# New slot tables for the engines of a two-layer attention and expert kernel, and a second set for its last two batches

## The chip, the core and the metric

The kernel runs on one core of one Trainium2 chip. The core has five engines with an instruction queue each, worked off in order: TensorE (PE, its weight loads shown as PEld), VectorE (DVE), ScalarE (ACT), GpSimd (POOL) and SyncE (SP, which here only issues DMAs). They meet only in semaphores. The metric is the device time of one launch in microseconds; lower is better.

## The reference, cut to what matters

```python
x = x + L0_xattn(layernorm(x), ctx)   # softmax(theta ctx . phi x) . g x, layer norm over all, relu, out_w, + ctx
x = x + L0_ffn(layernorm(x))          # base_w x + 2 of 8 low-rank experts (lora), gates by softmax
x = x + L1_xattn(layernorm(x), ctx)   # 8 heads of 32 rows: softmax(q k) v, keys and values from ctx
x = x + L1_moe(layernorm(x))          # router 512x64, 8 of 64 experts a row, silu(gate)*up, down, scatter-add
```

There are 16 batches of 256 rows by 512 columns, all float32.

## The kernel before, in words

**Two stages.** The first stage runs the first three layers and the routing, batch by batch, and writes each normed row with its 64 weights into the slots of its 8 experts in HBM (`slot_rows`). The second stage (from about 1222 us) runs over the 64 experts: it loads an expert's 256 slots and weights, multiplies them, and adds the results into `out_rows` in HBM.

**The order of the first stage.** It is written out in tables, one per engine. A table gives each event a position in slots. A batch has 32 slots: in slot n, TensorE does ("key", n), the product whose exponent ScalarE takes (`key_chunk`, profile line L665), and ("score", n+20), the product whose row maximum VectorE takes ahead of time (`score_chunk`, L656; maximum L1190). `schedule` turns tables into one list per engine, sorted by position; events of one position keep an order of kind and batch. Only the order counts: an engine does its list in order and waits at an event until its semaphores allow it.

- Preparation of batch b (tables `TENSOR`, `SCALAR`, `VECTOR`, `GPSIMD`, `SYNC`): an event stands at 32b - 64 + its number. `ctx` and `x` load the batch (L413, L404). `theta`, `phi`, `g`, `s0`-`s3` (L577), `t0`-`t3`, `lat`, `mean`, `o0`, `o1` are the first layer; `x0`, `x1`, `lora`, `b00`-`b13`, `gated`, `f0`, `f1` the second. `xn40`, `xn41`, `q_hi`, `q_lo`, `k_hi`, `k_lo` make the operands of the third. `k0`-`k3` and `q0`-`q3` on SP are three DMAs each that stack them for heads 0/4, 1/5, 2/6, 3/7 (L419); the first score of a head waits for its stacks.
- Two quads of 16 slots make a batch. When a quad's 16 scores are reduced, the maxima are turned (`max`, L689), split by ScalarE and VectorE, and SP copies them (`max_rows`, L429, 8 KB each) as two more rows of the stack. The quad's first key waits for both (`max_in`). `sums`, `turn`, `inv`, `add` finish a quad and add it to the batch's rows.
- Dispatch of batch b (tables `_OUT`, at 32(b+1) + number): `stats0`, `stats1`, `rstd`, `rows0`, `rows1` norm the finished rows (L1231), `x0`, `x1` (L720), `route` (L729), `exp`, `top0`-`top2`, `place`, `place0`-`place2` route them and give the slots (`slot_i`, L1290); 16 `send` events on POOL write the rows (indirect DMAs, L1431); `out` on SP writes the residual stream.
- Fills: slots of HBM that no row reaches must hold zeros. SP writes 577 KB for each of the 64 experts (`fill`, L463), at -18, -16.56, -15.13 ... with 1.44 slots between them, the last at 72.6.

**PSUM banks.** Banks 0 to 4 belong to keys, scores and weighted sums. All other events share banks 5 to 7; a planner in `build` walks TensorE's list and gives each stage the bank whose last reader stands earliest. A stage waits until that reader is done.

Of the kernel before, what the change touches and what calls it, by code (L numbers as in the profile page):

```python
# [31 lines left out]
class Count:  # L32
# [5 lines left out]
    def up(self, by=1):  # L38
# [5 lines left out]


PREPARE = 64
TENSOR = {"theta": 10.5, "phi": 10.5, "g": 12, "s0": 11, "t0": 18, "lat0": 20, "s1": 11, "t1": 19, "lat1": 23.25,
# [3 lines left out]
SCALAR = {"xn0": 8, "xn1": 9.25, "xn20": 34.75, "xn21": 34.75, "xn40": 42.5, "xn41": 42.5, "theta": 10.75,  # L51
# [4 lines left out]
VECTOR = {"stats0": 4.75, "stats1": 6, "s0": 11.25, "r0": 12.25, "s1": 11.25, "r1": 12.5, "s2": 11.5, "r2": 14,  # L56
# [27 lines left out]

def schedule(dims, prepare, tail, maxima, dispatch, core):

    B, HALF, NHEAD, C = dims["B"], dims["HALF"], dims["NHEAD"], dims["T"] // P
    H4 = NHEAD // HALF  # L90
    QUAD, SLOTS = C * H4, NHEAD * C
    AHEAD = LEAD * H4
    out = []
    if "fill" in core:
        out += [(FILL_FROM + n * FILL_SLOTS / dims["NEXP"] - PREPARE, 0, ("fill", n)) for n in range(dims["NEXP"])]
    for n in range(B * SLOTS):
        if "key" in core:
            out.append((n, 0, ("key", n)))
        if "score" in core:
            out.append((n - AHEAD, 1, ("score", n)))  # L100
        if "add" in core and n // H4 % C == 1:
            out.append((n + 1, 2, ("add", n)))
# [33 lines left out]
def build(nc, a, out, slots_dram, dims):  # L136
    B, HALF, T, L, NHEAD, DQ, NE, NEXP, CAP, TOPK, NRANK = (
        dims[k] for k in ("B", "HALF", "T", "L", "NHEAD", "DQ", "NE", "NEXP", "CAP", "TOPK", "NRANK"))
# [21 lines left out]
    tensor_order = schedule(dims, TENSOR, TENSOR_TAIL, TENSOR_MAX, TENSOR_OUT, ("key", "score", "weighted"))  # L160
    scalar_order = schedule(dims, SCALAR, SCALAR_TAIL, SCALAR_MAX, SCALAR_OUT, ("key",))
    vector_order = schedule(dims, VECTOR, VECTOR_TAIL, VECTOR_MAX, VECTOR_OUT, ("score",))
    gpsimd_order = schedule(dims, GPSIMD, {}, {}, GPSIMD_OUT, ("add",))
    sync_order = schedule(dims, SYNC, {}, SYNC_MAX, SYNC_OUT, ("fill",))

# [16 lines left out]
    with stack:  # L182
        def sem(name):
            return stack.enter_context(nc.semaphore(name))
# [51 lines left out]
        lat_rstd = sem("lat_rstd")  # L236
# [3 lines left out]
        gate_exp = sem("gate_exp")  # L240
# [33 lines left out]
        def A(name, shape, dt=F32):  # L274
            return sb(name, shape, dt, small)
# [31 lines left out]
        theta = A("theta", [P, T])  # L307
        phi = A("phi", [P, T])
# [3 lines left out]
        lat = theta  # L312
# [22 lines left out]
        top2 = A("top2", [P, HALF, 8])  # L335
# [5 lines left out]
        gated = A("gated", [P, HALF, NF])  # L341
# [1190 lines left out]
```

## Time and profile before

| | us |
|---|---|
| median of 3 runs | 1825.39 (1823.33 to 1825.6) |
| the profiled execution's own time | 1832.02 |
| its span | 1830.3 |
| TensorE busy | 1651.0 (90%) |
| VectorE, ScalarE, GpSimd busy | 1198.1, 1003.3, 964.8 |

The span runs from the first instruction of the program to its last. In the profile's forty slices TensorE is at 5 to 8 tenths in the first four (to 183 us), at 9 from there to 1098 us, at 6, 2 and 9 tenths in the three slices from 1144 us, and at 9 to the end.

### The profile page before, as it was taken

The numbers are of one execution on the slowest core, as the hardware profiler recorded it, in microseconds if no ns is written. First come the engines' busy times: TensorE is split into PE (matmuls) and PEld (weight loads), VectorE is DVE, ScalarE is ACT, GpSimd is POOL, SyncE is SP. The second block draws the span as 40 slices with busy tenths as digits, with TensorE's granted clock in tenths as the row PEclk, the third lists the DMA queues.
The fourth block names the chain that finished last, engine by engine and source line by source line (L and its number), as shares of the span: only waits on it lengthen the run. The fifth ranks groups of instructions, "written<-read, shape, count | busy, mean of one in ns | idle before, by whom it ended". The sixth has DMA issues, their size and how long they took to land. (4 is left out here: it accounts for less than half of the span.)

```text
span 1830.3 us, 26026 instructions
## 1 busy us (share of the span) xinstructions
PE 1651.0 (90%) x8576; PEld 1075.1 (59%) x8576; DVE 1198.1 (65%) x2706; ACT 1003.3 (55%) x1970; POOL 964.8 (53%) x882
## 2 busy tenths in 40 slices
PE   5878899999999999999999989629999999999994
PEld 2434454554554554554555544329888888888884
DVE  2555577777787777787787776317766666657662
ACT  3435556666656666656656644315555555555552
POOL 3121232563563563563564555756666666666665
PEclk8979999999999999999999999759999999999997
DMA  3679663533533533523431330159999999999985
GB/s 101 187 235 315 195 226 90 184 110 124 184 116 114 169 100 109 155 84 93 129 91 59 98 84 18 33 167 242 243 256 245 253 255 246 252 248 255 259 226 79
DMA packets 139732, 303.32 MB, mean 166 GB/s; under 512 B 27385, under 2 KB 29305, under 8 KB 139598
## 3 DMA queue, kind: packets, MB, share of 16 engines
q1 hardware_dynamic: 100686, 230.23, 40.4%
q0 software_dynamic: 38912, 71.43, 17.9%
q8 instruction: 69, 1.13, 0.3%
q14 instruction: 65, 0.53, 0.1%
HBM read 132.60 MB, written 155.91 MB: 158 GB/s over the span
## 5 line engine op out<-in xcount | busy, mean ns | idle before, releaser
L1190 DVE TENSOR_REDUCE max_col<-bank 128x1 f32<-128x512 f32 x512 | 345.0, 685 | 159.5 <-PE bank L656 157.0
L946 ACT ACTIVATE p_t<-bank 128x512 f32<-128x512 f32 x512 | 299.0, 596 | 198.0 <-PE bank L665 194.7
L1478 POOL DMA_INDIRECT out_rows<-y_slots,row_ids x128 | 228.7, 1787 | 203.9 <-DMA out_rows<-y_slots,row_ids 158.7
L1419 POOL TENSOR_TENSOR p_sum<-p_t 128x512 f32<-128x512 f32 x128 | 167.3, 1318 | 307.7 <-ACT p_t L946 306.6
L1431 POOL DMA_INDIRECT slot_rows<-row,slot_i x256 | 265.8, 1038 | 72.0 <-issue 71.9
L665 PE MATMUL bank<-q_stack,k_stack 98*128 98x512 f32 x512 | 274.3, 536 | 16.3 <-DMA q_stack<-max_lo 15.3
L656 PE MATMUL bank<-k_stack,q_stack 96*128 96x512 f32 x512 | 213.4, 418 | 22.9 <-issue 13.9
L665 PEld LDWEIGHTS bank<-q_stack,k_stack 98*128 98x128 f32 x512 | 98.4, 193 | 174.5 <-issue 152.1
L1468 POOL TENSOR_TENSOR down_lo<-down,down_hi 96x1024 fp32r<-96x1024 f32 x64 | 188.4, 2944 | 16.0 <-DVE down_hi L1350 16.0
L1319 DVE TENSOR_TENSOR x_slots_t_lo<-bank,x_slots_t_hi 128x512 fp32r<-128x512 f32 x128 | 88.3, 690 | 156.2 <-ACT x_slots_t_hi L1003 156.1
L785 PE MATMUL bank<-gate_up_hi,x_slots_t_hi 128*128 128x384 f32 x512 | 186.9, 365 | 0.7 <-DVE x_slots_t_lo L1319 0.5
L787 PE MATMUL bank<-gate_up_hi,x_slots_t_lo 128*128 128x384 f32 x512 | 175.8, 343 | 0.0
L786 PE MATMUL bank<-gate_up_lo,x_slots_t_hi 128*128 128x384 f32 x512 | 175.7, 343 | 0.0
L1023 ACT ACTIVATE y_slots<-bank,x_slots 128x512 f32<-128x512 f32 x128 | 88.1, 688 | 132.1 <-PE bank L809 132.1
L774 PE MATMUL bank<-ident,x_slots 128*128 128x128 f32 x512 | 80.7, 281 | 64.1 <-DMA x_slots<-slot_rows 64.1
L678 PE MATMUL bank<-p_t,v_t 128*32 128x512 f32 x1024 | 137.7, 610 | 0.0
L1340 DVE TENSOR_TENSOR gate_up_lo<-gate_up,gate_up_hi 128x768 fp32r<-128x768 f32 x128 | 132.2, 1034 | 7.0 <-ACT gate_up_hi L1033 7.0
L656 PEld LDWEIGHTS bank<-k_stack,q_stack 96*128 96x128 f32 x512 | 99.5, 194 | 62.8 <-issue 40.2
L637 PE MATMUL bank<-base_w,x_t 128*128 128x512 f32 x256 | 123.0, 603 | 0.0
L774 PEld LDWEIGHTS bank<-ident,x_slots 128*128 128x128 f32 x512 | 62.6, 143 | 89.7 <-DMA x_slots<-slot_rows 43.2
L1033 ACT CAST gate_up_hi<-gate_up 128x768 fp32r<-128x768 f32 x128 | 105.3, 824 | 15.1 <-DMA down<-in_down 15.1
L807 PE MATMUL bank<-down_hi,hidden_t_hi 96*128 96x512 f32 x256 | 112.0, 437 | 1.8 <-POOL down_lo L1468 1.8
(175 smaller groups left out, 3304.2 us busy)
## 6 DMA issues: line engine op xcount, KB each, us to landing
gate_up<-in_gate_up SPq DMA_DIRECT2D x64, 768.0 KB, 6.5
slot_rows<-row SPq DMA_DIRECT2D x64, 577.0 KB, 7.3
x_slots<-slot_rows SPq DMA_DIRECT2D x64, 577.0 KB, 4.5
k_stack<-prob SPq DMA_DIRECT2D x192, 128.0 KB, 2.4
down<-in_down SPq DMA_DIRECT2D x64, 384.0 KB, 7.4
q_stack<-x_t SPq DMA_DIRECT2D x128, 128.0 KB, 3.3
x<-in_x SPq DMA_DIRECT2D x16, 512.0 KB, 3.7
ctx<-in_ctx SPq DMA_DIRECT2D x16, 512.0 KB, 3.9
```

Of the source, the lines that this page charges most:

```text
L656: e.matmul(psum[2 + n % 2][:, :], q_st[b % 2][0:SK, head, c * P:(c + 1) * P], k_st[b % 2][0:SK, head, :], start=True, stop=True).then_inc( ...
L665: e.matmul(psum[n % 2][:, :], k_st[b % 2][0:SKM, head, j * P:(j + 1) * P], q_st[b % 2][0:SKM, head, :], start=True, stop=True).then_inc(fu ...
L774: m = e.transpose(psum[u % 2][:, c * P:(c + 1) * P], xe[i][:, s, c * P:(c + 1) * P], ident[:, :])
L785: e.matmul(bk[:, 0:2 * INNER], xt_hi[u % 3][:, c, :], gu_hi[nw][:, c, :], start=c == 0, stop=False)
L786: e.matmul(bk[:, 0:2 * INNER], xt_hi[u % 3][:, c, :], gu_lo[nw][:, c, :], start=False, stop=False)
L787: m = e.matmul(bk[:, 0:2 * INNER], xt_lo[u % 3][:, c, :], gu_hi[nw][:, c, :], start=False, stop=c == C - 1)
L946: e.activation(p_t[step % 2][:, h, :], psum[n % 2][:, :], ACT.Exp, scale=SCALE).then_inc(free[n % 2], 1)
L1190: e.tensor_reduce(max_col[quad % 2][:, h, c:c + 1], psum[2 + n % 2][:, :], X, ALU.max, negate=True).then_inc(free[2 + n % 2], 1)
L1419: e.tensor_tensor(p_sum[:, h, :], p_t[(step - 1) % 2][:, h, :], p_t[step % 2][:, h, :], ALU.add).then_inc(p_sum_ok, 1)
L1431: e.indirect_dma_start(out=slots_dram, in_=rows[b % 2][:, k, :], in_offset=None, out_offset=bass.IndirectOffsetOnAxis(ap=slot_i[b % 2][:, ...
L1468: e.tensor_tensor(dn_lo[nw][:, :, :], dn[i][:, :, :], dn_hi[nw][:, :, :].bitcast(F32), ALU.subtract).then_inc(dn_lo_ok, 1)
L1478: e.indirect_dma_start(out=out, out_offset=bass.IndirectOffsetOnAxis(ap=row_ids[e_ % NI][:, q, :].bitcast(U32), axis=0), in_=ye[e_ % NY][: ...
```

## The change

Every table gets new numbers. `SYNC` moves `x`, `ctx`, `q3`, `max` and `out` by 6.5 to 9 slots to the back, `k` and `q0`-`q2` hardly at all. A second set of dispatch tables (`_LATE`) holds for batches 14 and 15: their `x0` on TensorE stands at 74.5 instead of 41. `schedule` takes it as one more argument. No instruction is added or removed; `FILL_FROM` and the fills' positions stay. `GPSIMD_LATE` has rstd 42.25 and send 78.25.

```diff
-TENSOR = {... "s0": 11, "t0": 18, ... "s1": 11, "s2": 11.25, "s3": 13, ... "b02": 40.25, "gated": 40.5, "v0": 41.5, "v1": 42.75,
-          "theta": 10.5, "phi": 10.5, "g": 12 ...}
+TENSOR = {... "s0": 11.25, "t0": 14.75, ... "s1": 11.25, "s2": 11.25, "s3": 11.25, ... "b02": 41, "gated": 41, "v0": 41.75, "v1": 42.5,
+          "theta": 10, "phi": 10.5, "g": 12 ...}
-SCALAR = {... "xn40": 42.5, "xn41": 42.5, "theta": 10.75, "phi": 10.75, "n0": 12.75, "n3": 16.25, "k_hi0": 25.25, "k_hi1": 28, "q_hi0": 42.5 ...}
+SCALAR = {... "xn40": 42.5, "xn41": 42.5, "theta": 10.25, "phi": 11, "n0": 12.25, "n3": 13.25, "k_hi0": 38.5, "k_hi1": 38.75, "q_hi0": 42.5 ...}
-GPSIMD = {"rstd": 7.25, "res0": 9.5, "res1": 10.75, "lat_rstd": 28, "rstd2": 34.5, "rstd4": 42.25}
-SYNC = {"ctx": -11.75, "x": -5.5, "k0": 41.5, "k1": 42.5, "k2": 42.75, "k3": 42.75, "q0": 43, "q1": 43, "q2": 45.5,
-        "q3": 45.75}
+GPSIMD = {"rstd": 7.75, "res0": 10, "res1": 10, "lat_rstd": 28, "rstd2": 32, "rstd4": 42.25}
+SYNC = {"ctx": -5, "x": 2, "k0": 41, "k1": 41.25, "k2": 41.75, "k3": 42.5, "q0": 43, "q1": 43, "q2": 43, "q3": 52.25}
 
-TENSOR_OUT = {"x0": 41, "x1": 41, "route": 42, "place": 44}
-SCALAR_OUT = {"x0": 41.25, "x1": 41.75, "exp": 42.5}
-GPSIMD_OUT = {"rstd": 25, "send": 65}
-SYNC_OUT = {"out": 22}
+TENSOR_OUT = {"x0": 42.25, "x1": 42.5, "route": 43, "place": 46.25}
+SCALAR_OUT = {"x0": 42.5, "x1": 42.75, "exp": 43.5}
+GPSIMD_OUT = {"rstd": 22.25, "send": 67.5}
+SYNC_OUT = {"out": 31}
+
+LATE = 2
+TENSOR_LATE = {"x0": 74.5, "x1": 76, "route": 76.5, "place": 77.75}
+SCALAR_LATE = {"x0": 75, "x1": 76.25, "exp": 77}
+VECTOR_LATE = {"stats0": 34.25, "stats1": 36.5, "rows0": 46, "rows1": 48.5, "peak": 76.75, ... "place2": 78}
 ...
-SYNC_MAX = {"max": 5.75}
+SYNC_MAX = {"max": 13}
 ...
-        for what, o in dispatch.items():
+        for what, o in (dispatch if b < B - LATE else late).items():
```

## Rows read from the trace of the kernel before

**Rows 1.** Windows: us, busy us of PE, PEld, DVE, ACT, POOL, clock, DMA share, GB/s

```profile
76.00:106.00 30.00, 16.01 (x51) 8.07 (x50) 18.80 (x37) 7.86 (x15) 2.10 (x6) 0.77 1.03 360
300.00:1100.00 800.00, 780.17 (x4046) 413.86 (x4042) 605.67 (x1527) 493.66 (x968) 428.81 (x497) 0.99 0.39 116
1161.00:1222.00 61.00, 17.11 (x97) 13.92 (x95) 17.37 (x68) 8.23 (x19) 45.43 (x49) 0.58 0.25 72
1222.00:1831.00 609.00, 550.08 (x3072) 495.23 (x3072) 374.40 (x637) 319.25 (x638) 383.86 (x192) 0.95 0.91 236
```

**Rows 2.** Waits of PE, 40 to 300 us: total us, times, longest

```profile
PE bank L665 <- DMA q_stack<-max_lo: 15.3, 4, 8.2
```

**Rows 3.** Timeline of PE: start, us; idle before and releaser in brackets

```profile
105.76 0.77 PE L665 MATMUL bank<-q_stack,k_stack 98*128 98x512 f32 x1 [8.20 <-DMA q_stack<-max_lo]
...
150.60 0.76 PE L665 MATMUL bank<-q_stack,k_stack 98*128 98x512 f32 x1 [3.59 <-DMA q_stack<-max_lo]
...
222.49 0.77 PE L665 MATMUL bank<-q_stack,k_stack 98*128 98x512 f32 x1 [2.83 <-DMA q_stack<-max_lo]
```

**Rows 4.** Timeline of SP's DMA issues

```profile
76.09 5.47 SPq L463 DMA_DIRECT2D slot_rows<-row  x5
...
95.55 1.04 SPq L429 DMA_DIRECT2D q_stack<-max_hi  x1
...
133.51 0.59 SPq L419 DMA_DIRECT2D q_stack<-x_t  x1
...
145.22 1.14 SPq L429 DMA_DIRECT2D q_stack<-max_hi  x1
...
217.07 1.46 SPq L429 DMA_DIRECT2D q_stack<-max_hi  x1
```

**Rows 5.** Line L463 from 75 to 105 us: issues, and time from issue to landing

```profile
L463 SPq DMA_DIRECT2D slot_rows<-row x20: 507/1145/1843, 76.1 to 103.9; - x20
...
DMA to landing us min/median/max: 4.2/8.9/10.8
```

**Rows 6.** Line L429, the same, at 90 to 100 us

```profile
DMA to landing us min/median/max: 9.0/9.3/9.6
```

**Rows 7.** Line L429, the same, at 170 to 174 us

```profile
DMA to landing us min/median/max: 1.8/1.8/1.8
```

**Rows 8.** Timeline around the first score of a batch

```profile
416.76 0.79 PE L665 MATMUL bank<-q_stack,k_stack 98*128 98x512 f32 x1
...
418.67 0.47 PE L656 MATMUL bank<-k_stack,q_stack 96*128 96x512 f32 x1 [1.11 <-issue]
...
422.40 1.02 PE L577 MATMUL bank<-phi,theta 128*128 128x512 f32 x2
```

**Rows 9.** Timeline before it, of another batch

```profile
814.23 1.08 ACT L976 COPY x_t<-bank 128x512 f32<-128x512 f32 x2 [1.96 <-PE bank L720]
...
819.44 1.12 ACT L932 CAST x_t<-xn 128x512 fp32r<-128x512 f32 x2
...
820.46 1.88 PE L562 MATMUL bank<-xn,phi_w 128*128 128x512 f32 x4
```

**Rows 10.** Group of keys, 300 to 1100 us: busy us, mean ns, idle before

```profile
L665 PE MATMUL bank<-q_stack,k_stack 98*128 98x512 f32 x376 | 201.5, 536 | 0.0
```

**Rows 11.** Line L665 from 60 to 260 us: ns shortest, median, longest

```profile
L665 PE MATMUL bank<-q_stack,k_stack x72: 392/500/803, 105.8 to 258.3; 98*128 98x512 f32 x72
```

**Rows 12.** Timeline of the end of the first stage

```profile
1163.68 1.09 PE L720 MATMUL bank<-ident,row 128*128 128x128 f32 x8
...
1165.95 1.97 PE L729 MATMUL bank<-route_w,x_t 128*128 128x64 f32 x16 [1.19 <-ACT x_t L976]
...
1175.52 0.17 DVE L1290 TENSOR_SCALAR slot_i<-slot 128x16 int32<-128x16 f32 x1
...
1179.27 1.07 POOL L1431 DMA_INDIRECT slot_rows<-row,slot_i  x1 [0.19 <-issue]
...
1183.61 3.64 PE L729 MATMUL bank<-route_w,x_t 128*128 128x64 f32 x16 [0.72 <-issue]
```

More of the change, by code:

```diff
@@ L46 @@
 PREPARE = 64
-TENSOR = {"theta": 10.5, "phi": 10.5, "g": 12, "s0": 11, "t0": 18, "lat0": 20, "s1": 11, "t1": 19, "lat1": 23.25,
[3 rows of a table removed]
-SCALAR = {"xn0": 8, "xn1": 9.25, "xn20": 34.75, "xn21": 34.75, "xn40": 42.5, "xn41": 42.5, "theta": 10.75,
[4 rows of a table removed]
-VECTOR = {"stats0": 4.75, "stats1": 6, "s0": 11.25, "r0": 12.25, "s1": 11.25, "r1": 12.5, "s2": 11.5, "r2": 14,
[3 rows of a table removed]
-GPSIMD = {"rstd": 7.25, "res0": 9.5, "res1": 10.75, "lat_rstd": 28, "rstd2": 34.5, "rstd4": 42.25}
-SYNC = {"ctx": -11.75, "x": -5.5, "k0": 41.5, "k1": 42.5, "k2": 42.75, "k3": 42.75, "q0": 43, "q1": 43, "q2": 45.5,
-        "q3": 45.75}
@@ L64 @@
-TENSOR_OUT = {"x0": 41, "x1": 41, "route": 42, "place": 44}
-SCALAR_OUT = {"x0": 41.25, "x1": 41.75, "exp": 42.5}
-VECTOR_OUT = {"stats0": 4.75, "stats1": 22.75, "rows0": 25.75, "rows1": 25.75, "peak": 42.25, "top0": 42.75,
-              "top1": 42.75, "top2": 42.75, "place0": 45.75, "place1": 46, "place2": 46}
-GPSIMD_OUT = {"rstd": 25, "send": 65}
-SYNC_OUT = {"out": 22}
-TENSOR_TAIL = {"sums0": -2.5, "sums2": -1.75, "sums1": 1, "turn": 11, "inv": 15.75}
-SCALAR_TAIL = {"heads": 4.5, "sums": 6.5, "expand": 12.75}
@@ L73 @@
-VECTOR_TAIL = {"turn": 11.25, "inv": 16, "add": 17.5}
+TENSOR = {"theta": 10, "phi": 10.5, "g": 12, "s0": 11.25, "t0": 14.75, "lat0": 20, "s1": 11.25, "t1": 16.75,
[3 rows of a table added]
+          "lora": 39.5, "gated": 41}
+SCALAR = {"xn0": 8.5, "xn1": 9.75, "xn20": 34, "xn21": 34.75, "xn40": 42.5, "xn41": 42.5, "theta": 10.25, "phi": 11,
[4 rows of a table added]
+VECTOR = {"stats0": 4.75, "stats1": 5.5, "s0": 11.5, "r0": 12, "s1": 11.5, "r1": 12, "s2": 11.5, "r2": 12, "s3": 11.5,
[3 rows of a table added]
+GPSIMD = {"rstd": 7.75, "res0": 10, "res1": 10, "lat_rstd": 28, "rstd2": 32, "rstd4": 42.25}
@@ new lines @@
+SYNC = {"ctx": -5, "x": 2, "k0": 41, "k1": 41.25, "k2": 41.75, "k3": 42.5, "q0": 43, "q1": 43, "q2": 43, "q3": 52.25}
+TENSOR_OUT = {"x0": 42.25, "x1": 42.5, "route": 43, "place": 46.25}
+SCALAR_OUT = {"x0": 42.5, "x1": 42.75, "exp": 43.5}
+VECTOR_OUT = {"stats0": 20.25, "stats1": 20.5, "rows0": 25.5, "rows1": 25.5, "peak": 43.25, "top0": 43.75, "top1": 44,
+              "top2": 44, "place0": 46.5, "place1": 46.5, "place2": 46.5}
+GPSIMD_OUT = {"rstd": 22.25, "send": 67.5}
+SYNC_OUT = {"out": 31}
@@ new lines @@
+LATE = 2
+TENSOR_LATE = {"x0": 74.5, "x1": 76, "route": 76.5, "place": 77.75}
+SCALAR_LATE = {"x0": 75, "x1": 76.25, "exp": 77}
+VECTOR_LATE = {"stats0": 34.25, "stats1": 36.5, "rows0": 46, "rows1": 48.5, "peak": 76.75, "top0": 77.25, "top1": 77.5,
+               "top2": 77.5, "place0": 78, "place1": 78, "place2": 78}
+GPSIMD_LATE = {"rstd": 42.25, "send": 78.25}
+SYNC_LATE = {"out": 37.5}
+TENSOR_TAIL = {"sums0": -2.25, "sums2": -2.25, "sums1": 0.25, "turn": 11, "inv": 15.5}
+SCALAR_TAIL = {"heads": 4.75, "sums": 7, "expand": 14.75}
@@ L75 @@
+VECTOR_TAIL = {"turn": 11.5, "inv": 18, "add": 18.5}
 TENSOR_MAX = {"max": 1.25}
@@ L77, with schedule @@
 VECTOR_MAX = {"max_lo": 1.75}
-SYNC_MAX = {"max": 5.75}
-WEIGHTED = 6.25
+SYNC_MAX = {"max": 13}
+WEIGHTED = 6.5
 LEAD = 5
 FILL_FROM, FILL_SLOTS = 46, 92
-def schedule(dims, prepare, tail, maxima, dispatch, core):
+def schedule(dims, prepare, tail, maxima, dispatch, late, core):
     B, HALF, NHEAD, C = dims["B"], dims["HALF"], dims["NHEAD"], dims["T"] // P
@@ L158, in build @@
     BC = NHEAD * C
[L160 to L164, printed above, removed]
+    tensor_order = schedule(dims, TENSOR, TENSOR_TAIL, TENSOR_MAX, TENSOR_OUT, TENSOR_LATE, ("key", "score", "weighted"))
+    scalar_order = schedule(dims, SCALAR, SCALAR_TAIL, SCALAR_MAX, SCALAR_OUT, SCALAR_LATE, ("key",))
+    vector_order = schedule(dims, VECTOR, VECTOR_TAIL, VECTOR_MAX, VECTOR_OUT, VECTOR_LATE, ("score",))
+    gpsimd_order = schedule(dims, GPSIMD, {}, {}, GPSIMD_OUT, GPSIMD_LATE, ("add",))
+    sync_order = schedule(dims, SYNC, {}, SYNC_MAX, SYNC_OUT, SYNC_LATE, ("fill",))
     read_at = {}
```

20 rows, old and new, of tables (SCALAR, TENSOR, VECTOR) are left out of this document.

## The prediction, made before the result was known

> **What bounds the kernel now.** I first cut the span into windows [rows 1]. From 300 to 1100 us TensorE is busy 780 of 800 us at a granted clock of 0.99: it bounds the steady part, and 19.8 us of idle time in some 12 batches, 1.65 us a batch, are what a better order could take from it outright. Waits inside a matmul's modelled length are not in that: keys last 536 ns in the mean [rows 10], and with nothing to hold them about 400 (the shortest 392 [rows 11]). The second stage is at 0.91 of the DMA engines from 1222 us on; nothing of it is touched. Two stretches are bounded by something else. From 76 to 106 us TensorE is busy 16 of 30 us while the DMA engines show 1.03 and 360 GB/s: the fills saturate them. From 1161 to 1222 us POOL is busy 45 of 61 us with 49 instructions, the sends, and TensorE 17.
>
> Then I read what TensorE waits for at the start. Its longest kind of wait there, 15.3 us in four times, is for the small DMAs of the quad's maxima [rows 2], and it stands before the first key of quads 0, 1 and 3 (8.20, 3.59, 2.83 us) [rows 3].
>
> **Step 1, the start: SP's order against the fills.** I merged both sets of positions. In the steady part SP's order stays what it is: max, k, q, max, ctx, out, x. Only against the fills, which keep their positions, do the moved events change place. `max` of quad 0 goes from 0.75 to 8 and so behind five more fills (n = 14 to 18); of quad 1 from 16.75 to 24, five more (25 to 29); of quad 3 from 48.75 to 56, five more. `q3` goes from just behind `q2` to behind five fills for batch 0 and six for batches 1 and 2.
>
> What five fills cost: a fill is 577 KB, at 360 GB/s [rows 1] 1.64 us, so five are 8.2 us. That such a backlog stands before a later DMA is in the trace: 20 fills, issued from 76.1 to 103.9 us, took 4.2 us from issue to landing at first and up to 10.8 [rows 5], and the 8 KB of quad 0's maxima issued in their midst took 9.0 to 9.6 us [rows 6], where the same DMAs took 1.8 us with nothing ahead [rows 7].
>
> - Quad 0: SP came to `max` at 95.55 us [rows 4], its key started at 105.76 [rows 3]. Behind five more fills it lands 8.2 us later. The fills begin earlier by `q3`'s three DMAs, 1.9 us of issue, but these then stand behind five fills and add 1.1 us of transfer: 8.2 + 1.1 - 1.9 = 7.4 us. `q3` itself lands at about 87 us instead of 77, which holds score 3 and all behind it for some 9 us, but the maxima are then ready at about 100 us, before SP gets to them at about 102: it costs nothing on top.
> - Quad 1: `q0` is issued at 133.5 us [rows 4]; `q0` to `q2` take nine issues, 5.8 us; then six fills (9.8 us) and `q3` (1.1), three fills (4.9): with the 3.5 us to the first landing the maxima land at about 158.6 - 1 = 157.6 us on the old time base, where the key started at 150.6 [rows 3]: 7.0 us.
> - Quad 2: `max` was issued into an empty queue [rows 7], and its key came some 10 us later; five more fills are gone by then. Nothing.
> - Quad 3: as quad 1, nine fills and `q3` behind `q2`: 8.1 us behind the old 222.49 us [rows 3].
> - Quad 4: SP stands at `x` of batch 4 for rows of batch 0 before it, in both orders, with four fills behind; nothing.
>
> Sum 22.5 us. TensorE takes its list in order, so each pause shifts all behind it. Some of it comes back, since ScalarE, VectorE and POOL catch up in a pause and later small waits for them shrink; the quads' other waits are 0.7 to 2 us each. I take 3.5 us back: +19. Bounds: 0, if DMAs of 8 KB get past the backlog, and +26, if nothing comes back and the lower clock after each pause (0.77 in 76 to 106 us [rows 1]) lasts longer.
>
> The Trainium skill bears on this in DMA: Bandwidth & Descriptors, section Queues, rings and completion order: each DMA engine consumes descriptors in ring order, but completion is not first in, first out per issuing engine, since a later DMA on few engines need not wait for an earlier one's other engines. The 9.0 to 9.6 us [rows 6] speak for the queue and against overtaking. By overtaking the sum would be 1828, by the queue 1846.
>
> **Step 2, the steady batches.** The first score of a batch waits for `q0`, 1.11 us at 418.67 us [rows 8], and `s3`, two matmuls with 0.86 us from start to start, stood behind it; now it stands ahead and fills the wait. `v0` no longer stands behind `x0` and `x1` of the dispatch, which saves 0.4 us. So -1.3 us a batch at best. Against it: the planner now gives `x0` and `x1` of the dispatch the same bank, where they had two. ScalarE reads `x0` only behind `xn40`, `xn41`, `q_hi0` and `q_hi1`, which end at 819.44 + 1.12 = 820.56 us [rows 9]; with a copy of 0.6 us the bank is free at 821.2, and TensorE, with the phi group (1.88 us at 820.46 [rows 9]) now drawn forward, would be there at 819.9: +1.3. `route`, the `turn` that VectorE reads only behind `peak`, and `s1` and `s2`, whose banks hang on these reads, come 0.7 us late: +2.0 at worst. `rstd4` on POOL has five operations of about 1.3 us between it and the last add as before (two sends and two residual adds and a norm, for three sends, one add and a norm), so `q0` comes no sooner. The moved `t0` to `t3`, `n0` to `n3` and `k_hi` lie where neither view shows TensorE waiting: zero, hidden by keys and scores; without that cover a 0.7 us operation each. Over 13 batches the ends are -17 and +26 us. I take 0, since the two wait places are of one size.
>
> **Step 3, the end.** POOL sends 48 times (batches 13, 14 and 15) from 1157 us on, 1.28 us each, with only one gap: 1.75 us behind the send at 1179.27 [rows 12]. So nothing that makes slots sooner counts; what makes them late does. Before, the dispatch of batch 14 stood ahead of quad 31's `turn`: transposes at 1163.68 us, slots at 1175.7, and POOL came to batch 14's sends at 1179.27 [rows 12]. Now `turn`, `inv` and the tail's copies come first, so the transposes start at about 1168.3: slots at 1175.7 + 4.6 - 0.6 (the `turn` that stood in between) = 1179.7. The route took 1.97 us at 1165.95 and 3.64 at 1183.61 with the clock at its lower level [rows 12], and it would now run at 1170 or later: 1181.4. POOL waits 0.4 to 2.1 us. Batch 15's rows come before its sends are due. `rstd` of batch 14 is now amid the sends, which moves it and adds none. I take +1.5; the ends are -1.5 (the gap of 1.75 us goes) and +3.5.
>
> **The sum.** 19 + 0 + 1.5 = +20.5 us: the profiled execution's span of 1830.3 would be 1850.8 and its own time of 1832.0 1852.5. It stood 6.6 us above the median of the runs; on the median's base, 1825.4 + 20.5 = 1846 us.
>
> **Rivals.**
> - The steady part packs better: the pauses' cost of step 1 stays, but the new order takes the 1.65 us of idle time a batch [rows 1] and a third of the stretch in the keys (376 times 136 ns, 51 us [rows 10]): over 13.5 batches 22 + 19 = 41 us. It would be 1846 - 41 + bank waits of some 15 = 1820, faster. For it: `s3` in the wait of `q0`. Against it: the bank chain. It decides from 1.6 us a batch.
> - The backlog doesn't count for 8 KB: with 1.8 us to landing [rows 7] and SP at `max` at 102.5 us quad 0's key would start at about 105, as before; the start costs at most 2 us, the whole 1828, which is no change. The page named in step 1 allows this much, since completion needn't follow the order of issue.
> - The bank chain has no cover: step 2 at +1.5 us a batch, +20, so 1866.
> - The end gets shorter, since batch 15's rows no longer stand behind batch 14's routing in quad 31's tail: POOL is the bound, so at most the 1.75 us. This changes no sign.
>
> **How the numbers follow.** A change of 0.2%, 3.7 us, is about what can be told here. Forecast (1834 to 1858) 0.55; packs better 0.17; no backlog 0.08; bank chain 0.15; else, slower by other waits, 0.05. So faster 0.17, same 0.08, slower 0.75. The range takes the forecast's own, half of the faster case and most of the bank chain: 1822 to 1865.
>
> **What would show it.** Waits for q_stack<-max_lo before 300 us of 35 us and more instead of 15.3; first keys at about 113, 165 and 245 us; L429 issued at 102 us; a first batch of sends of batch 14 with POOL idle for slot_i before it; batches 5 to 15 within 1 us of 66 to 68 us each. Wrong it is if the first key starts before 108 us, or if a steady batch changes by over 1.5 us.

## The result and the profile after

| | us | ratio to the kernel before |
|---|---|---|
| before, median of 4 runs | 1824.9 (1823.3 to 1825.6) | |
| after, median of 4 runs | 1847.1 (1841.7 to 1855.8) | 1.0127 (0.95 interval 1.0085 to 1.017) |
| after, profiled execution | 1841.7, span 1840.0 | |

The change made the kernel 22 us slower; 1846 was predicted. The two profiled executions lie only 9.7 us apart in their spans, since that of before stood above its median and that of after below. So each trace is cut at the last send of the first stage: it starts at 1220.9 us before and at 1241.4 after, 20.5 us later. What is left behind it is 609.3 us before and 598.5 after; no instruction of the second stage differs, and the last section shows that this part scatters.

Windows of the changed kernel, columns as in [rows 1]:

```profile
76.00:106.00 30.00, 18.36 (x44) 9.77 (x44) 17.20 (x32) 3.33 (x6) 0.88 (x3) 0.66 1.03 353
300.00:1100.00 800.00, 784.78 (x4067) 412.36 (x4066) 602.36 (x1531) 492.15 (x978) 408.58 (x485) 1.00 0.38 114
```

The DMA engines are as full at the start as they were (1.03 in both), and in the steady part TensorE is busy 785 of 800 us instead of 780. What TensorE waits for between 40 and 300 us has changed; of [rows 2] the one line is now two:

```profile
PE bank L664 <- issue: 22.3, 3, 8.3
PE bank L673 <- DMA q_stack<-max_lo: 13.7, 4, 4.4
```

L664 is the score, L673 the key. Where these waits stand, in the timeline of TensorE (before in [rows 3]):

```profile
81.54 1.19 PE L664 MATMUL bank<-k_stack,q_stack 96*128 96x512 f32 x2 [7.16 <-issue]
...
108.18 0.76 PE L673 MATMUL bank<-q_stack,k_stack 98*128 98x512 f32 x1 [4.28 <-DMA q_stack<-max_lo]
...
156.46 0.77 PE L664 MATMUL bank<-k_stack,q_stack 96*128 96x512 f32 x1 [6.87 <-issue]
...
161.65 0.76 PE L673 MATMUL bank<-q_stack,k_stack 98*128 98x512 f32 x1 [4.42 <-DMA q_stack<-max_lo]
...
235.70 0.77 PE L664 MATMUL bank<-k_stack,q_stack 96*128 96x512 f32 x1 [8.28 <-issue]
...
241.45 0.76 PE L673 MATMUL bank<-q_stack,k_stack 98*128 98x512 f32 x1 [4.12 <-DMA q_stack<-max_lo]
```

The three pauses ahead of a score are those of the first score that needs `q3`, in batches 0, 1 and 2: 22.3 us where the kernel before has 2.6. The profile names no releaser for them ("issue"); that they are waits for `q3` is shown by a_q3_back below, where they fall to 1.9 us. And SP's issues (before in [rows 4]):

```profile
62.45 0.59 SPq L427 DMA_DIRECT2D q_stack<-x_t  x1
...
74.38 1.28 SPq L427 DMA_DIRECT2D q_stack<-x_t  x1
...
77.13 1.40 SPq L427 DMA_DIRECT2D q_stack<-x_t  x1
...
98.06 1.08 SPq L437 DMA_DIRECT2D q_stack<-max_hi  x1
```

The first of these lines is the first copy of `q0` of batch 0. No fill stands ahead of it in either kernel, so the change of SP's order does not reach it. In the kernel before it stands at

```profile
67.78 0.58 SPq L419 DMA_DIRECT2D q_stack<-x_t  x1
```

So this execution was 5.3 us ahead before the first fill was issued. That is scatter: after_again, a_no_late and a_no_late_again are the same program up to there, and have this copy at 65.3, 62.7 and 66.4 us. Where the start is measured below, it is therefore counted from this copy too.

For the rest one table does, read from the traces of all kernels: where the turned maxima (`max` on TensorE) of four quads and the last send start, in us. Quad 4 is the end of the start, quads 5 to 30 are the steady part, and the last column but one is the end of the stage, from quad 30's maxima to the last send.

| kernel | quad 0 | quad 4 | quad 5 | quad 30 | last send | steady | end |
|---|---|---|---|---|---|---|---|
| before | 89.9 | 242.1 | 285.7 | 1115.2 | 1220.9 | 829.5 | 105.7 |
| after | 96.5 | 260.3 | 304.1 | 1137.3 | 1241.4 | 833.2 | 104.1 |
| a_sp_before | 90.3 | 240.2 | 284.5 | 1118.9 | 1222.6 | 834.4 | 103.7 |
| b_sp_after | 98.1 | 263.6 | 309.6 | 1136.5 | 1242.5 | 826.9 | 106.0 |
| a_q3_back | 91.6 | 269.0 | 315.6 | 1147.6 | 1251.7 | 832.0 | 104.1 |
| a_max_back | 100.5 | 251.5 | 294.6 | 1140.3 | 1246.7 | 845.7 | 106.4 |
| a_fills_grouped | 90.5 | 220.3 | 268.0 | 1173.2 | 1291.2 | 905.2 | 118.0 |
| a_fills_again | 91.2 | 220.5 | 268.1 | 1174.2 | 1292.4 | 906.1 | 118.2 |
| b_fills_grouped | 87.9 | 218.1 | 263.1 | 1090.0 | 1205.9 | 826.9 | 115.9 |
| b_fills_again | 87.8 | 218.1 | 263.1 | 1089.2 | 1206.8 | 826.1 | 117.6 |
| after_again | 99.1 | 259.5 | 303.8 | 1205.9 | 1324.2 | 902.1 | 118.3 |
| a_sp_gated | 91.1 | 241.1 | 286.3 | 1190.7 | 1309.1 | 904.4 | 118.4 |
| a_no_late, a_no_late_again | 96.8, 99.5 | 260.1, 262.7 | 304.1, 306.8 | 1199.3, 1212.2 | 1319.5, 1332.2 | 895.2, 905.4 | 120.2, 120.0 |

After against before: +18.4 us up to quad 5, +3.7 from there to quad 30, and -1.6 to the last send. Their sum is the 20.5. The 18.4 hold 23.7 us of delay behind the first copy of `q0` and the 5.3 us that this execution was ahead at it. The kernel before has one trace only, from the first group of runs; all kernels are compared with that one.

### The profile page after: what moved, and what is told of

It is laid out like the page before. It is cut to its first block, busy times and chain, and to the rows that moved or that the text cites. A ratio compares the mean times of both kernels' runs of the same rounds, so it can differ in the third digit from the quotient of the medians.

```text
span 1840.0 us, 26037 instructions
## 1 busy us (share of the span) xinstructions
PE 1647.4 (90%) x8576; PEld 1067.8 (58%) x8576; DVE 1191.8 (65%) x2706; ACT 994.2 (54%) x1970; POOL 947.6 (52%) x882
## 4 chain that ended last, share of the span: by engine, by line
PE 44%; DMA 20%; issue 12%; POOL 10%; SPq 6%; DVE 6%; ACT 3%; POOLq 0%; ACTq 0%; DVEq 0%
DMA out_rows<-y_slots,row_ids 16%; PE bank L673 5%; PE bank L686 5%; PE bank L664 5%; POOL slot_rows L1439 4%; PE bank L606 3%; SPq L427 3%; SPq L471 2%; PE bank L708 2%; PE bank L645 2%; POOL p_sum L1427 2%; PE bank L585 2%; PE bank L650 2%; PE bank L599 2%; PE bank L701 2%
## 5 line engine op out<-in xcount | busy, mean ns | idle before, releaser
L1198 DVE TENSOR_REDUCE max_col<-bank 128x1 f32<-128x512 f32 x512 | 340.9, 683 | 160.9 <-PE bank L664 159.0
L1486 POOL DMA_INDIRECT out_rows<-y_slots,row_ids x128 | 221.9, 1733 | 200.5 <-DMA out_rows<-y_slots,row_ids 157.6
L1427 POOL TENSOR_TENSOR p_sum<-p_t 128x512 f32<-128x512 f32 x128 | 162.9, 1280 | 294.4 <-ACT p_t L954 292.9
L1439 POOL DMA_INDIRECT slot_rows<-row,slot_i x256 | 260.2, 1016 | 79.1 <-issue 78.1
L673 PE MATMUL bank<-q_stack,k_stack 98*128 98x512 f32 x512 | 268.2, 525 | 16.0 <-DMA q_stack<-max_lo 13.7
L664 PE MATMUL bank<-k_stack,q_stack 96*128 96x512 f32 x512 | 216.4, 425 | 33.3 <-issue 25.8
L1476 POOL TENSOR_TENSOR down_lo<-down,down_hi 96x1024 fp32r<-96x1024 f32 x64 | 188.6, 2948 | 15.3 <-DVE down_hi L1358 15.3
L673 PEld LDWEIGHTS bank<-q_stack,k_stack 98*128 98x128 f32 x512 | 98.6, 193 | 157.0 <-issue 131.9
L664 PEld LDWEIGHTS bank<-k_stack,q_stack 96*128 96x128 f32 x512 | 101.1, 198 | 72.5 <-issue 47.6
L1348 DVE TENSOR_TENSOR gate_up_lo<-gate_up,gate_up_hi 128x768 fp32r<-128x768 f32 x128 | 136.0, 1063 | 7.0 <-ACT gate_up_hi L1041 7.0
```

The source lines that it names most:

```text
L664: e.matmul(psum[2 + n % 2][:, :], q_st[b % 2][0:SK, head, c * P:(c + 1) * P], k_st[b % 2][0:SK, head, :], start=True, stop=True).then_inc( ...
L673: e.matmul(psum[n % 2][:, :], k_st[b % 2][0:SKM, head, j * P:(j + 1) * P], q_st[b % 2][0:SKM, head, :], start=True, stop=True).then_inc(fu ...
L1198: e.tensor_reduce(max_col[quad % 2][:, h, c:c + 1], psum[2 + n % 2][:, :], X, ALU.max, negate=True).then_inc(free[2 + n % 2], 1)
L1427: e.tensor_tensor(p_sum[:, h, :], p_t[(step - 1) % 2][:, h, :], p_t[step % 2][:, h, :], ALU.add).then_inc(p_sum_ok, 1)
L1439: e.indirect_dma_start(out=slots_dram, in_=rows[b % 2][:, k, :], in_offset=None, out_offset=bass.IndirectOffsetOnAxis(ap=slot_i[b % 2][:, ...
L1476: e.tensor_tensor(dn_lo[nw][:, :, :], dn[i][:, :, :], dn_hi[nw][:, :, :].bitcast(F32), ALU.subtract).then_inc(dn_lo_ok, 1)
```

## The experiments

Names with a_ start from the changed kernel, with b_ from the kernel before. a_sp_before, b_sp_after, a_q3_back and a_max_back shared a chip (before: median 1829.8). The two fills_grouped, a_no_late and a_sp_gated ran on another (before: 1845.0), the four named again on a third (before: 1831.6). The kernel before scatters by 11 to 22 us within each of these groups, so the traces decide more than the times.

**a_sp_before.**

```diff
-SYNC = {"ctx": -5, "x": 2, "k0": 41, ... "q2": 43, "q3": 52.25}
+SYNC = {"ctx": -11.75, "x": -5.5, "k0": 41.5, ... "q2": 45.5, "q3": 45.75}
-SYNC_OUT = {"out": 31}   -SYNC_MAX = {"max": 13}
+SYNC_OUT = {"out": 22}   +SYNC_MAX = {"max": 5.75}
```

> The changed kernel with SP's three tables (SYNC, SYNC_MAX, SYNC_OUT) as before; the other engines keep the new ones, and batches 14 and 15 their second set. Theory: the place of q3 and of the maxima's copies among the fills is the whole cost, some 18 us by the shift of quad 4 between the two traces (242.1 to 260.3 us at its turned maxima). Then the time is 1847 - 18 = 1829 (1825 to 1833), and no score waits over 2 us before 260 us. Rival, the other engines' tables cost as well: it stays above 1836. Rival, they gain and SP's order hid it (the waits ahead of scores fell from 15.8 to 7.2 us between 300 and 1100 us): below 1822.

Measured: 1832.1, ratio 1.0014 (0.9991 to 1.0037). Waits of TensorE, 40 to 300 us:

```profile
PE bank L674 <- DMA q_stack<-max_lo: 14.1, 4, 6.3
PE bank L665 <- issue: 1.9, 2, 1.7
```

The start is that of the kernel before (quad 4 at 240.2 against 242.1; counted from the first copy of `q0`, 174.6 against 174.3), and with it the 20 us are gone. The other tables leave +4.9 us in the steady part and -2.0 in the end.

**b_sp_after.** The reverse: these three tables of the changed kernel in the kernel before.

> The kernel before with SP's three tables from the changed one, nothing else. Theory: 1825 + 18 = 1843 (1839 to 1848), with waits of about 7, 7 and 8 us ahead of the score that needs q3 in batches 0, 1 and 2 and the turned maxima of quad 4 at about 260 us instead of 242. Rival, other tables cost too: below 1836. That SP's order costs only together with the new order of the other engines would show as no change, 1825.

Measured: 1852.1, ratio 1.0114 (1.0066 to 1.0161), 22 us above the kernel before.

```profile
PE bank L655 <- issue: 24.7, 3, 10.4
PE bank L664 <- DMA q_stack<-max_lo: 15.7, 4, 5.6
```

SP's order alone makes the loss of the start, with either order of the other engines. Quad 4 is 21.5 us late here and 18.2 in the changed kernel; counted from the first copy of `q0` it is 24.2 and 23.5, so the other tables make no difference that can be told.

**a_q3_back.** Only `"q3": 52.25` to `45.75` in the changed kernel.

> The changed kernel with q3 at 45.75 as before, so ahead of the fills; the maxima stay behind five more fills. The working of the prediction says that the maxima alone set the first key: it then starts at about 112 us, the waits for the maxima rise from 13.7 to some 35 us, those of scores for q3 go, and the time stays at 1847 (1842 to 1852). Rival, the 22 us of waits for q3 are the cost and the maxima's place costs nothing: 1847 - 18 = 1829.

Measured: 1862.5, ratio 1.0162 (1.0107 to 1.0217). Moving `q3` forward brought no gain. The last send starts 10.3 us later than in the changed kernel's trace, but 6.1 of these stand already at the first copy of `q0` (68.5 instead of 62.4 us), which the edit doesn't reach; and the ratio's interval overlaps that of the changed kernel. The waits ahead of the scores are gone (1.9 us instead of 22.3). The pauses ahead of the keys:

```profile
PE bank L673 <- DMA q_stack<-max_lo: 44.2, 4, 16.0
```

```profile
115.22 0.77 PE L673 MATMUL bank<-q_stack,k_stack 98*128 98x512 f32 x1 [16.00 <-DMA q_stack<-max_lo]
...
170.76 0.77 PE L673 MATMUL bank<-q_stack,k_stack 98*128 98x512 f32 x1 [13.29 <-DMA q_stack<-max_lo]
...
249.67 0.76 PE L673 MATMUL bank<-q_stack,k_stack 98*128 98x512 f32 x1 [12.85 <-DMA q_stack<-max_lo]
```

These three keys are 7.8, 9.7 and 10.0 us longer on hold than in [rows 3]. That is the prediction's own mechanism, bare, and about as large as its 8.2 us for five fills. Most of it is that SP comes to the copies later, since each fill's issue takes some 1.2 us of SP's own time here:

```profile
76.79 12.15 SPq L471 DMA_DIRECT2D slot_rows<-row  x10
```

SP issued `max_lo` 7.7 us later than before at quad 0 (104.37 instead of 96.64 us, of which 0.7 stand already at `q0`), and 7.4 and 6.6 us later at quads 1 and 3, counted from the batch's own `q0`. The rest is the way from the issue to the key: 10.9 us instead of 9.1 at quad 0, 7.0 and 7.3 instead of 4.2 and 3.9 at the others.

**a_max_back.** Only `"max": 13` to `5.75` in the changed kernel.

> The changed kernel with the maxima's copies at 5.75 as before, so ahead of five fills; q3 stays behind five or six. If the maxima's place alone costs, 1829. If q3's place alone costs, 1847, with 22 us of waits ahead of scores. If each delays by its own, the waits for q3 stay at 22 us and those for the maxima fall from 13.7 to about 5, since the backlog drains while TensorE stands at q3: 1847 - 9 = 1838 (1834 to 1842).

Measured: 1850.2, ratio 1.0121 (1.0065 to 1.0177).

```profile
PE bank L664 <- issue: 21.9, 3, 8.5
```

The maxima are no longer among TensorE's waits there, and the 22 us for `q3` stand. At quad 4 the shift is 9.4 us (11.4 counted from the first copy of `q0`): each place delays by its own, as the third of the written expectations had it. The time missed that expectation because of the steady part, where this kernel loses 16 us against before: with `max` at 5.75 and `q3` at 52.25, SP reaches `q3` of the next batch only behind the maxima of the quad before it, at 641.46 us behind 640.22 in this timeline, and scores then wait in nearly every batch, 10.1 us in 12 times between 330 and 1110 us, against 3.5 in 4 for the changed kernel:

```profile
640.22 0.56 SPq L437 DMA_DIRECT2D q_stack<-max_hi  x1
...
641.46 0.65 SPq L427 DMA_DIRECT2D q_stack<-x_t  x1
```

```profile
PE bank L664 <- issue: 10.1, 12, 1.7
```

Between quads 5 and 30 TensorE is idle for 28.7 us here and 19.0 in the changed kernel. So this edit changed two things, and only its first 250 us are a clean test.

**b_fills_grouped and b_fills_again** (the same kernel, in the second and the third group).

```diff
-        out += [(FILL_FROM + n * FILL_SLOTS / dims["NEXP"] - PREPARE, 0, ("fill", n)) for n in range(dims["NEXP"])]
+        at = [p for p, n in FILL_AT for _ in range(n)]
+        out += [(at[n], 0, ("fill", n)) for n in range(dims["NEXP"])]
+FILL_AT = [(-18, 8), (0.8, 14), (16.8, 12), (32.8, 12), (48.8, 12), (64.8, 6)]
```

> The kernel before with its 64 fills grouped in the same way: 8 behind q3 of batch 0, then 14, 12, 12, 12, 6 right behind the maxima of quads 0 to 4. By the theory of the backlog the 15.3 us of waits for the maxima fall to about 5, the first key starts at about 99 us instead of 105.8: 1825 - 10 = 1815 (1810 to 1820), and within 6 us of the changed kernel with grouped fills. Rival: a group of 12 to 14 holds SP for some 15 us, so that x and ctx come late and give the gain back: 1825.

> The kernel before with grouped fills, once more, beside the others. On its first runs it was 25 us below the kernel before, of which its stage one accounts for 15 in the profile (last send at 1205.9 instead of 1220.9 us). If the 15 are the fills' and the rest scatter, it is 10 to 20 us below the kernel before here: 1805 to 1815 where that is at 1825. If it was the chip alone, no difference.

Measured: 1819.6 against 1845.0, ratio 0.986 (0.9812 to 0.9909), and 1809.3 against 1831.6, ratio 0.9883 (0.9821 to 0.9945). This version beats the kernel before in both groups, by 1.2 to 1.4%. The waits for the maxima, 15.3 us in [rows 2], are

```profile
PE bank L666 <- DMA q_stack<-max_lo: 2.1, 1, 2.1
```

and quad 4 comes 24.0 us sooner (22.0 counted from the first copy of `q0`), which is more than the 13 us of waits. One quad shows why. First the kernel before from quad 1's maxima to quad 2's, then the grouped one:

```profile
139.90:170.30 30.40, 25.80 (x124) 12.27 (x123) 12.40 (x26) 16.60 (x32) 5.03 (x4) 0.89 0.99 337
```

```profile
130.40:153.10 22.70, 22.70 (x125) 11.00 (x122) 12.23 (x26) 16.50 (x32) 5.04 (x4) 1.00 0.93 315
```

With the same matmuls, TensorE is idle for 4.6 us less and its busy time is 3.1 us shorter, at a granted clock of 1.00 instead of 0.89 (means of the stretch, of the two levels 1.2 and 2.4 GHz); 25.80 times 0.89 is 23.0, so the clock accounts for the difference in busy time. The clock is at its lower level in one piece of this stretch, 150.1 to 156.9 us, and that piece begins as the 3.6 us pause ahead of the key at 150.60 [rows 3] ends. So this pause is paid twice, as idle time and in the clock. Of the 24 us, 15.0 (14.1 in the repeat) arrive at the last send: the end takes 116 to 118 us instead of 105.7. POOL, which the prediction found busy with sends almost without a gap from 1157 us on, now stands for want of the last batches' rows:

```profile
1162.86 0.22 POOL L1372 TENSOR_SCALAR row_rstd<-row_mv 128x2 f32<-128x2 f32 x1 [6.82 <-DVE row_mv L1074]
```

**a_fills_grouped and a_fills_again.** The same grouping in the changed kernel, FILL_AT at -11.7, 8.05, 24.05, 40.05, 56.05, 72.05.

> The changed kernel with the same 64 fills in another place: 8 behind q3 of batch 0, and 14, 12, 12, 12, 6 right behind the maxima's copies of quads 0 to 4, so that in batches 1 to 3 no fill stands between a batch's q0 and its maxima. If the backlog of fills is what delays q3 and the maxima, the 36 us of waits for both fall to under 10 and turned maxima of quad 4 come before 240 us instead of 260: 1847 - 18 - 8 = 1821 (1815 to 1828). If SP's places of q3 and maxima cost in themselves, by other rows of SP, it stays at 1847.

> The changed kernel with grouped fills, the same as before. Stalls a matter of the chip: on one without them the time is that of the first forecast for it, 1821 (1815 to 1828), which is some 25 below the changed kernel of the same runs. Stalls made by the grouping: it is slow again, 1900, with the changed kernel at 1847.

Measured: 1903.5, ratio 1.0315 (1.0283 to 1.0348), and 1889.9, ratio 1.0329 (1.0257 to 1.0401). The times miss what was expected by some 80 and 70 us, but at quad 4 (220.3, 220.5 us) the kernel is where it was expected, 40 us ahead of the changed one and 2 from the kernel before with the same grouping. SP's places of `q3` and the maxima cost next to nothing in the start once no backlog of fills stands ahead. What was lost came behind quad 5.

**after_again.** The changed kernel itself, unchanged, in the third group.

> The changed kernel itself once more. In three runs of kernels with the new tables of the other engines TensorE stood still 5 to 10 us at the routing's 16 products of a batch (there VectorE and ScalarE waited 120.5 us in 20 times for the row maximum of the routing between 300 and 1150 us, against 32.5 us in 18 for the changed kernel's own profile), and each time took 60 to 90 us more. If that hangs on the chip that runs it, and on the new order of TensorE, the changed kernel does the same where those do, and is at 1847 or 20 above the kernel before of the same runs where they don't. If it hangs on the edits of those three (fills grouped, second set off, the gates' places), the changed kernel is 20 above the kernel before whatever they do.

Measured: 1934.6, ratio 1.0576 (1.0506 to 1.0646), so 103 us above the kernel before, where the first runs had 22. It is the same program with the same start (quad 5 at 303.8 against 304.1 us), and its steady part is 69 us longer. The first time it leaves the other trace (POOL, VectorE and TensorE):

```profile
361.73 1.09 POOL L1439 DMA_INDIRECT slot_rows<-row,slot_i  x1 [0.30 <-issue]
...
363.17 1.93 PE L737 MATMUL bank<-route_w,x_t 128*128 128x64 f32 x16
...
364.93 1.08 PE L585 MATMUL bank<-phi,theta 128*128 128x512 f32 x2
365.68 0.97 POOL L1439 DMA_INDIRECT slot_rows<-row,slot_i  x1 [0.30 <-issue]
...
369.51 0.97 POOL L1439 DMA_INDIRECT slot_rows<-row,slot_i  x1 [0.30 <-issue]
...
371.34 0.29 DVE L1246 TENSOR_REDUCE r_max<-bank 128x2 f32<-128x128 f32 x1 [7.72 <-remote]
```

The router's 16 products end at 365.1 us by the trace's model, and VectorE, which waits for them alone, starts at 371.34: TensorE's signal came 6.2 us late. TensorE then stands itself, 6.05 us here, since its next product needs a bank that VectorE reads only behind `r_max`. What VectorE and ScalarE waited for ahead of `r_max` and its reader, 300 to 1150 us, first here, then in the first profile of the same kernel:

```profile
  remote: 135.9, 20
```

```profile
  PE bank L737: 32.5, 18
```

It hangs on the new order of the engines together with the chip or the hour: a_fills_grouped, a_no_late and a_sp_gated have it, and the repeats; the changed kernel's first profile and the four kernels of the first group have it nowhere, VectorE starting 0.04 us behind the products each time; and b_fills_grouped and b_fills_again, run beside them, have it in none of the steady batches. POOL differs at that place. In the new order a row of eight sends stands back to back around the router's products. In the old one, as here in b_fills_again, single sends stand between adds:

```profile
381.49 1.30 POOL L1389 TENSOR_TENSOR x<-x,ctx 128x512 f32<-128x512 f32 x1
382.95 1.00 POOL L1432 DMA_INDIRECT slot_rows<-row,slot_i  x1 [0.17 <-issue]
...
383.45 1.90 PE L730 MATMUL bank<-route_w,x_t 128*128 128x64 f32 x16
384.02 0.22 POOL L1372 TENSOR_SCALAR row_rstd<-row_mv 128x2 f32<-128x2 f32 x1
...
385.38 0.29 DVE L1239 TENSOR_REDUCE r_max<-bank 128x2 f32<-128x128 f32 x1 [1.04 <-PE bank L730]
```

In after_again the batch before the first sends (router done at 297.9 us) is undisturbed. The 11 that follow, to 1109 us, are late by 1.5 to 7.4 us, 54.2 us together, of the 69 that its steady part is longer. SP's copies of `q` stand beside the router in the new order too, which would be a rival. But the one late signal of b_fills_again, 2.25 us at 1149.9 us (2.09 in b_fills_grouped), falls in the end of the stage, where POOL has sends in a row and SP issues nothing between 1138 and 1162 us. Against it, the first profile of the changed kernel has the same rows of sends and none late, and of after_again's last four routings, with sends around them as well, none is. That sends take part is an inference from these coincidences; no run took them away.

**a_no_late and a_no_late_again.** `LATE = 2` to `LATE = 0`.

> The changed kernel with the second set of dispatch tables off (LATE = 0), so batches 14 and 15 by the common ones. The prediction's third step gives the second set +1.5 us: the last send would start at about 1240 instead of 1241.4 us, and POOL would not wait for slot_i at the first send of batch 14. Rival: the second set gains, as quad 31's turned maxima come 4 us earlier by the traces (the shift falls from 22.0 to 17.9 us there): then the last send starts at 1245. Either is too small for the times; the trace decides. Time 1845 to 1851.

> The changed kernel with the second set of dispatch tables off, once more. Without stalls in the steady part the last send starts within 4 us of the changed kernel's (1241.4 us in its first profile), and the sign tells what the second set is worth: 1.5 us earlier by the prediction's third step, 3.6 us later by its rival. With stalls again and none in the changed kernel, the edit would be their cause.

Measured: 1935.8, ratio 1.051 (1.0462 to 1.0559), and 1934.0, ratio 1.0568 (1.0489 to 1.0648). The times say nothing on the edit: the changed kernel itself is at 1934.6 beside the second. The ends don't settle it either. They take 120.2 and 120.0 us without the second set and 118.0 to 118.4 with it (after_again, a_sp_gated and the two grouped ones), but without it the router's signal of batch 14 comes 5.8 and 4.9 us late, at 1260.1 and 1273.5 us, and with it none does in the end. So the second set's worth in an execution without late signals stays open, its sign too. The rival's reason is wrong, though: quad 31's maxima follow quad 30's by 20.8 us without the second set too, and by 20.7 with it.

**a_sp_gated.** a_sp_before with `lora`, `gated`, `gate_exp` and the gates at their old places.

> The changed kernel with SP's tables of before, and lora, gated, gate_exp and the gates at their places of before too. In the steady part the new order has a wait of 5.8 us in 11 times for gated_t ahead of the product that adds the gated half, which the kernel before has not. Theory: that wait is what the new tables cost there; between quads 5 and 30 the shift against the kernel before, which was +4.9 us with SP's old tables alone, falls to 0 or below, and the stage ends near 1218. Rival: the wait is taken from others of the same slot; the shift stays within 1 us of +4.9.

Measured: 1913.1 in one run, in a group with the late signals, so the shift at quad 30 can't be read. Only the wait can be. First a_sp_before, then a_sp_gated, 300 to 1100 us:

```profile
L651 PE MATMUL bank<-lora_out,gated_t 65*128 65x512 f32 x48 | 25.7, 616 | 5.7 <-ACT gated_t L923 5.7
...
L640 PE MATMUL bank<-ident,gated 128*65 128x128 f32 x24 | 4.7, 276 | 1.3 <-DVE gated L1175 1.3
```

```profile
L651 PE MATMUL bank<-lora_out,gated_t 65*128 65x512 f32 x44 | 22.5, 592 | 0.0
...
L640 PE MATMUL bank<-ident,gated 128*65 128x128 f32 x22 | 4.8, 298 | 7.0 <-DVE gated L1175 7.0
```

Together the two lines are 7.0 us in both: the wait moved one product forward and stayed as long, where the kernel before has 1.1 us in all. So the places of these events don't make the wait. What the wait costs can't be read from this run.

## Why the prediction held, step by step

**Step 1, +19.** Measured +18.2 at quad 4 and +18.4 at quad 5, and a_sp_before with b_sp_after show that SP's order is the cause. But the profiled execution was 5.3 us ahead of that of before when SP issued the first copy of `q0`. The next table counts from the issues instead: from the first copy of `q0` of a batch to the first key of the quad, and, in the last column, from the first of all to quad 4. All in us.

| kernel | first `q0` at | batch 0, quad 0 | batch 1, quad 1 | batch 2, quad 3 | to quad 4 |
|---|---|---|---|---|---|
| before | 67.8 | 38.0 | 17.1 | 16.8 | 174.3 |
| a_sp_before | 65.6 | 38.6 | 17.0 | 18.0 | 174.6 |
| after | 62.4 | 45.7 | 24.8 | 26.1 | 197.8 |
| after_again | 65.3 | 45.3 | 24.7 | 24.4 | 194.2 |
| a_no_late | 62.7 | 46.4 | 25.3 | 24.8 | 197.4 |
| a_no_late_again | 66.4 | 45.5 | 25.3 | 26.2 | 196.3 |
| b_sp_after | 65.1 | 46.2 | 25.1 | 24.6 | 198.5 |
| a_q3_back | 68.5 | 46.7 | 27.3 | 26.7 | 200.5 |
| a_max_back | 65.7 | 41.4 | 20.7 | 21.9 | 185.7 |

So the account per place was right: 7.4, 7.0 and 8.1 us were predicted, and 7.7, 7.7 and 9.3 are measured in the changed kernel. Its first keys came at 108.18, 161.65 and 241.45 us where 113, 165 and 245 stood, 3 to 5 us early each; the early start covers that. The first one is only 0.18 us above the prediction's own sign of being wrong, 108 us; counted from `q0` it is clear of it.

Two things were wrong. One is the 3.5 us taken off because some delay would come back: quad 4 is 23.5 us late counted from `q0`, 19.9 to 24.2 in the five executions with the new order of SP, and their mean of 22.5 is the sum before anything was taken off. The total of +19 came right because the early start stood in for the give-back; that is luck. The other is where TensorE waits. The prediction had the waits for the maxima rise to 35 us beside some 9 us that scores would wait for `q3`; they fell to 13.7. The waits for `q3` (22.3 us) and for the maxima together are 36.0. That `q3`'s late landing "costs nothing on top" holds at the first keys: with `q3` ahead of the fills (a_q3_back) they come no sooner, and TensorE stands at the key for what it stood at the score.

The two delays cover each other: `q3` alone makes quad 4 11.4 us late (a_max_back), the maxima alone 26.2 (a_q3_back), both together 19.9 to 24.2. That the maxima alone cost more than both is not shown: it rests on one trace, 2.0 us above the highest of five that are themselves 4.3 apart. That an 8 KB DMA queues behind the fills, and doesn't pass them, is shown by a_q3_back: with five more fills ahead its keys stand 13 to 16 us. For the Trainium skill's rule in DMA: Bandwidth & Descriptors, section Queues, rings and completion order, this means that here the consumption in ring order decides, and no copy is seen to profit from the freedom in completion.

**Step 2, 0.** Measured +3.7. The expected gain is there: waits ahead of scores fell from 15.8 us to 7.2 between 300 and 1100 us. The feared bank chain is not: TensorE's idle time ahead of the `x0` and `x1` of the dispatch is 0.9 us in 88 products. A new wait that was not named is there too: the product of the gated half now waits for its transpose.

```profile
L664 PE MATMUL bank<-k_stack,q_stack 96*128 96x512 f32 x382 | 154.2, 404 | 7.2 <-issue 3.5 <-DMA q_stack<-x_t 2.6
...
L650 PE MATMUL bank<-lora_out,gated_t 65*128 65x512 f32 x46 | 24.7, 617 | 5.8 <-ACT gated_t L922 5.8
...
L728 PE MATMUL bank<-ident,row 128*128 128x128 f32 x88 | 13.5, 276 | 0.9
```

But the loss does not show in TensorE's idle time. Between quads 5 and 30, first before, then after:

```profile
285.70:1115.20 829.50, 808.29 (x4197) 426.69 (x4197) 627.72 (x1575) 513.61 (x1005) 438.42 (x506) 0.99 0.38 114
```

```profile
304.10:1137.30 833.20, 814.18 (x4207) 426.82 (x4204) 623.44 (x1586) 506.09 (x1004) 426.70 (x506) 0.99 0.38 114
```

TensorE is idle for 2.2 us less (19.0 instead of 21.2) and busy for 5.9 us more with the same work. In three traces with the old tables of the other engines (before, b_sp_after, b_fills_again) it is busy for 807.0 to 808.3 us of this part, in three with the new ones (after, a_sp_before, a_q3_back) for 812.9 to 814.2. Some 1.7 us of the 5.9 are the clock: the granted clock is at half, the 1.2 GHz level, for 13.7 us of this part after (1107 to 1121) and for 10.2 us before (560 to 563 and 1092 to 1099). The rest lies inside the modelled lengths of the products, which step 2 did not add up; which products hold it, and why, stays open. Nor did any case hold a signal of TensorE that comes late, which in after_again made this step +73 us.

**Step 3, +1.5.** Measured -1.6 in all. The wait named for it is there, 0.75 us ahead of batch 14's first send at 1199.09 us; the gap of 2 us behind that send is in both traces (1.97 and 2.08 us):

```profile
1199.09 1.16 POOL L1439 DMA_INDIRECT slot_rows<-row,slot_i  x1 [0.75 <-DVE slot_i L1298]
```

Against it stands a wait that the sum didn't look for, because it lies ahead of 1157 us. It is in the kernel before alone:

```profile
1151.11 4.99 POOL L1419 TENSOR_TENSOR p_sum<-p_t 128x512 f32<-128x512 f32 x4 [3.62 <-ACT p_t L946]
```

The term was meant for the second set. a_sp_before, which has that set and the old order of SP, has an end of 103.7 us, and the kernels with the old tables have 105.7 and 106.0 (before, b_sp_after), so the new tables of the other engines together make the end 2 us shorter. What the second set alone does to it is not shown.

**The sum.** 19 + 0 + 1.5 was predicted and 18.4 + 3.7 - 1.6 measured, to the same 20.5. The mechanism of step 1 is shown, and its size too; that the sum agrees to the tenth is luck. Counted from `q0`, step 1 is 4.7 us larger than predicted, which the early start of the execution hides, and the two others are off by +3.7 and -3.1, which nearly cancel. That the medians' difference of 22.2 agrees is partly luck of the runs, as after_again shows.

## What to carry to other kernels

Put large transfers that nobody waits for right behind the small one that somebody waits for, never ahead of it, and count for each DMA that is moved back what is then ahead of it in the queue. Two delays behind one queue are not added: the first hides the second, so taking one away can gain nothing. And a table of where a few fixed events start, one row for each kernel, tells changes of some 3 us in the steady part and 2 in the end, where the times of the runs scatter by 20. It must be counted from an event just ahead of the change: from the start of the execution the same program scattered by 4 us before the change could act.

## What the runs showed of the hardware

The issue of a DMA on SP takes longer when the DMA engines are full: `q3`'s three took 1.28 to 1.40 us each from 74.38 us on, behind fills, where `q0`'s take 0.6. Fills are not needed for it: at 369.51 us of the same trace, 105 us behind the last fill and beside POOL's sends, a copy of 128 KB took 1.57 us, with the DMA engines busy at 0.89 from 362 to 375 us.

TensorE's signal at the end of the router's products came up to 7.4 us late in the steady part of after_again, and in a_fills_grouped at 401.6 us the router's signal and that of the next product, 0.6 us apart in issue, came within 0.05 us of each other at 409.2. TensorE's records show no pause inside these products. The same program ran without it (1847) and with it (1935). Whether it is the chip, and by what path sends could hold it up, is open.

The second stage, DMA at 0.95 of its engines, takes 597 to 614 us from the last send with the same instructions. Windows of 540 us and the waits for the slots, first the changed kernel, then b_fills_grouped:

```profile
1260.00:1800.00 540.00, 514.93 (x2930) 464.00 (x2929) 360.19 (x612) 304.25 (x611) 352.64 (x179) 0.99 0.95 252
```

```profile
PE bank L782 <- DMA x_slots<-slot_rows: 24.9, 25, 2.7
```

```profile
1225.00:1765.00 540.00, 504.68 (x2847) 453.53 (x2846) 349.41 (x595) 296.99 (x595) 347.72 (x175) 0.98 0.95 247
```

```profile
PE bank L775 <- DMA x_slots<-slot_rows: 35.4, 29, 2.8
```

At an equal share of busy DMA time one moves 252 GB/s and the other 247, 2% apart, and TensorE's waits differ by 10.5 us. It is not the kernel: the same program took 598.5 us in after and 609.1 in after_again, 613.7 in b_fills_grouped and 600.8 in b_fills_again. The 10.8 us by which this part was shorter in the profile of after than in that of before are most of the 12.5 by which the spans' difference of 9.7 falls short of the medians' 22.2.
